# Value copies by ScalarE and early score pairs inside the projections of a decoder layer

## The reference, cut to what matters

```python
result, ch_bias, n = _chunk_decompose(hidden_states)   # chunks of 64 rows: int4 values, per-channel bias
def proj(w_orig, w_dq_t, b):                           # w_dq_t: int4 weight, one scale s for an output channel
    y = result @ w_dq_t + ch_bias @ w_orig.T
    return y.reshape(-1, H)[:n] + b
Q = (proj(q_weight, WQ, q_bias) * scaling);  K = proj(k_weight, WK, k_bias);  V = proj(v_weight, WV, v_bias)
attn = jnp.einsum('bqhd,bkhd->bhqk', Q, K)
probs = jax.nn.softmax(attn, axis=-1)
...                                                    # probs @ V, then the output projection, quantised again
```

## Time and profile before

| what | value |
|---|---|
| median of the runs | 1018.01 us |
| the profiled execution | 1018.22 us, span 1016.2 us |
| PE busy | 769.0 us (76%) |
| DVE busy | 803.1 us (79%) |
| ACT busy | 603.2 us (59%) |
| POOL busy | 85.5 us (8%) |

### The profile page before, as it was taken

How to read it: one execution, slowest core, us unless ns; L and a number is a source line. 1 busy time by engine, 2 the same in 40 slices (tenths; PEclk the granted TensorE clock), 3 DMA queues, 4 the chain that set the end, 5 groups by cost and what they waited for, 6 DMA issues and landing times.

```text
span 1016.2 us, 15370 instructions
## 1 busy us (share of the span) xinstructions
PE 769.0 (76%) x5167; PEld 320.0 (31%) x5167; DVE 803.1 (79%) x1099; ACT 603.2 (59%) x1002; POOL 85.5 (8%) x204
## 2 busy tenths in 40 slices
PE   1548895999999999999963643555555539999997
PEld 0422231222222222222221113433434424444443
DVE  7899999899999999999599998868977884622111
ACT  5829231798888888888804513765666665853000
POOL 1210001000000000001000000000000340000101
PEclk9868897799999999999985675767766859999999
DMA  8500384121212111211030000200002940000000
GB/s 293 203 1 1 124 276 148 39 56 50 59 49 58 51 55 50 56 50 50 19 132 0 1 0 4 75 25 21 1 12 94 331 148 8 1 0 1 32 21 32
DMA packets 45732, 66.69 MB, mean 66 GB/s; under 512 B 8940, under 2 KB 23276, under 8 KB 45176
## 3 DMA queue, kind: packets, MB, share of 16 engines
q1 hardware_dynamic: 44408, 61.92, 19.0%
q0 software_dynamic: 1280, 4.20, 1.3%
HBM read 42.50 MB, written 19.14 MB: 61 GB/s over the span
## 4 chain that ended last, share of the span: by engine, by line
PE 49%; DVE 27%; ACT 11%; issue 6%; DMA 3%; POOL 1%; SPq 0%; ACTq 0%; POOLq 0%; DVEq 0%
PE PS L1364 11%; PE PS L1573 8%; PE PS L1584 8%; PE PS L1381 6%; PE PS L1333 6%; ACT slab L1681 4%; PE PS L1300 2%; PE PS L1501 2%; DVE SWV L883 2%; ACT HB L1672 2%; DMA slab<-in_L_ffn_w 2%; DVE mn L716 2%; DMA slab<-in_x 1%; DVE slab L809 1%; DVE slab L808 1%
## 5 line engine op out<-in xcount | busy, mean ns | idle before, releaser
L1681 ACT ACTIVATE slab<-PS 128x512 f32<-128x512 f32 x512 | 275.9, 595 | 58.8 <-PE PS L1381 51.3
L883 DVE TENSOR_REDUCE SWV<-PS 128x2 f32<-128x1024 f32 x256 | 300.6, 1217 | 12.6 <-PE PS L1333 10.2
L1364 PE MATMUL PS<-slab,HB 128*32 128x256 f32 x2048 | 164.3, 393 | 9.9 <-ACT HB L1672 9.6
L1381 PE MATMUL PS<-slab 50*128 50x512 f16 x512 | 125.3, 387 | 2.5
L1333 PE MATMUL PS<-slab 48*128 48x512 f16 x512 | 104.3, 404 | 11.2 <-DVE SWV L883 10.2
L1573 PE MATMUL PS<-slab 128*128 128x512 f16 x384 | 86.0, 387 | 1.7 <-DVE slab L1187 1.4
L1584 PE MATMUL PS<-slab 128*128 128x512 f16 x384 | 83.0, 379 | 0.0
L1364 PEld LDWEIGHTS PS<-slab,HB 128*32 128x32 f32 x2048 | 41.6, 108 | 91.1 <-issue 64.9
L1219 DVE SCALAR_TENSOR_TENSOR WOT<-PS,cmax,WOT 128x512 f32<-128x512 f32 x8 | 6.0, 750 | 69.8 <-PE PS L1584 69.8
L1333 PEld LDWEIGHTS PS<-slab 48*128 48x128 f16 x512 | 24.7, 93 | 114.0 <-issue 95.7
L1213 DVE SCALAR_TENSOR_TENSOR slab<-HB,cmax,slab 128x512 f16<-128x512 f32 x32 | 23.8, 750 | 43.6 <-ACT slab L1778 43.6
(11 more groups left out here) (308 smaller groups left out, 1194.7 us busy)
## 6 DMA issues: line engine op xcount, KB each, us to landing
slab<-in_L_ffn_w SPq DMA_DIRECT2D x2, 4096.0 KB, 14.8
q_split<-slab SPq DMA_DIRECT2D x24, 256.0 KB, 2.7
k_split<-slab SPq DMA_DIRECT2D x24, 256.0 KB, 2.7
slab<-q_split SPq DMA_DIRECT2D x64, 96.0 KB, 2.5
slab<-k_split SPq DMA_DIRECT2D x64, 96.0 KB, 2.5
slab<-in_x SPq DMA_DIRECT2D x4, 1024.0 KB, 12.1
slab<-HB SPq DMA_DIRECT2D x128, 32.0 KB
slab<-in_fside_BxS2xS SPq DMA_DIRECT2D x4, 1024.0 KB, 5.6
```

What stands on the lines that cost most here:

```text
L883: nc.vector.tensor_reduce(NM[:, ring].rearrange("p (a x) -> p a x", a=2)[:, :, x], PS[:, bank:bank + 2, :], AX.X, ALU.max, negate=True).th ...
L1364: ins = nc.tensor.matmul(PS[32 * h:32 * h + 32, 6, cols], VST[:, r % 2, k, h, :], PROB[:, k, h, cols], start=k == half == 0, stop=k == KB ...
L1381: nc.tensor.matmul(PS[:, st_bank(2 * s + a), :], KP[rows, r, p, P * k:P * k + P], QP[rows, r, p, :], start=True, stop=True).then_inc(st_re ...
L1681: nc.scalar.activation(PROB[:, k, 2 * a + p], PS[:, st_bank(t), :], ACT.Exp, scale=score_scale).then_inc(probs, 1)
```

## The change

- The value copy of each unit goes from VectorE to ScalarE, behind its split. It multiplies by the chunk's scale only. The channel scale goes into the context's normalisation, which becomes an operation with a scalar column (`scalar_tensor_tensor`). `SWV` as a row of scales is no longer made; its space still holds the maxima, and `identh` too, which VectorE now makes ahead of the projections.
- The 15 score pairs go into the projections: none in units 0 to 4, one in units 5 to 10, two in 11 to 14, one in 15 (`PAIRS_AT`). A unit's first pair stands ahead of its query/key matmuls, the second behind them; VectorE's maxima stand the same way around its scaling. All of them use banks 4 and 5, so a pair waits until the one before is reduced.
- For that the queries and keys have two bank pairs instead of three: unit u waits until unit u - 2 is scaled, not u - 3.
- Item 0's maxima are turned in unit 14, into bank 7.
- SyncE loads items 0 and 1 behind the stores of unit 2 instead of 4.

```diff
-        identh = slab[2][:, 0:64].bitcast(F16)
...
+        identh = SWV[:, 208:272].bitcast(F16)
...
         def qk_banks(u):
-            return 2 * (u % 3)
+            return 2 * (u % 2)
+        EARLY_BANK, TURN_BANK = 4, 7
+        EARLY_PAIRS = [(n // 8, n % 8) for n in range(8 + FIRST)]
+        PAIRS_AT = [0] * 5 + [1] * 6 + [2] * 4 + [1]
+        TURN_AT = 14
+        def early_pairs(u):
+            first = sum(PAIRS_AT[:u])
+            return list(enumerate(EARLY_PAIRS))[first:first + PAIRS_AT[u]]
...
             for u in range(NT):
                 store_split(u)
-                if u == 4:
+                if u == 2:
                     sp.wait_ge(kp_ready, 1)
...
-                if m >= 2:
-                    diagonal(DGS[:, m - 2], sw[:, m], dg_ready)
+                if m == 3:
+                    diagonal(DGS[:, 0], sw[:, m], dg_ready)
...
-                dve.wait_ge(swi_out, 3)
+                dve.wait_ge(swi_out, 1)
...
+            nc.vector.tensor_copy(identh, identf[:, :]).then_inc(identh_ready, 1)
+            def maxima_of_pair(j, x, ring, bank):
+                dve.wait_ge(s_ready, 8 * j + x + 1)
+                nc.vector.tensor_reduce(NM[:, ring].rearrange("p (a x) -> p a x", a=2)[:, :, x], PS[:, bank:bank + 2, :], AX.X,
+                                        ALU.max, negate=True).then_inc(s_free, 1)
+                if x == 7:
+                    dve.wait_ge(s_free, 8 * j + 8)
+                    nm = NM[:, ring].rearrange("p (a x) -> p a x", a=2)
+                    wait(dve, mt_ready, j)
+                    nc.vector.tensor_scalar(MS_PARTS[:, 0], nm, 1.0 / ROW_UNIT, None, ALU.mult).then_inc(ms_ready, 1)
+                    dve.wait_ge(ms_ready, 2 * j + 1)
+                    nc.vector.scalar_tensor_tensor(MS_PARTS[:, 1], nm, 1.0 / ROW_UNIT, MS_PARTS[:, 0], ALU.mult,
+                                                   ALU.subtract).then_inc(ms_ready, 1)
+            def turned_maxima(j, ring, bank):
+                dve.wait_ge(mt_ready, j + 1)
+                wait(dve, mrow_in[ring % 2], 16 * (j - ring % 2))
+                nc.vector.tensor_copy(MT[:, ring % 2], PS[0:32, bank, 0:64].bitcast(F16)).then_inc(mt_copied, 1)
             def rest(u):
                 dve.wait_ge(qk_h, u + 1)
                 nc.vector.tensor_tensor(SPLIT[:, u % 3, 1], XF[u % 3], SPLIT[:, u % 3, 0], ALU.subtract).then_inc(qk_l, 1)
             for u in range(NT):
                 half, m, o = u // 8, u % 2, u % 8 // 2
+                early = early_pairs(u)
+                for _, (j, x) in early[:1]:
+                    maxima_of_pair(j, x, j, EARLY_BANK)
                 dve.wait_ge(qk_mm, u + 1)
                 if u >= 3:
                     dve.wait_ge(qk_l, u - 2)
                 ps = PS[:, qk_banks(u):qk_banks(u) + 2].rearrange("p a (n k) -> p (a n) k", k=CHUNK)
                 nc.vector.tensor_tensor(by_chunk(XF[u % 3]), ps, bc(AQ[:, m, o, 16 * half:16 * half + 16]),
                                         ALU.mult).then_inc(qk_scaled, 1)
-                dve.wait_ge(v_mm, u + 1)
-                nc.vector.scalar_tensor_tensor(V[:, u // KB, :, u % KB], PS[:, 6 + u % 2].rearrange("p (g c) -> p g c", g=NG),
-                                               s0col[:, u:u + 1], SWV[:, :].rearrange("p (g c) -> p g c", g=NG),
-                                               ALU.mult, ALU.mult).then_inc(v_scaled, 1)
+                for _, (j, x) in early[1:]:
+                    maxima_of_pair(j, x, j, EARLY_BANK)
+                if u == TURN_AT:
+                    turned_maxima(0, 0, TURN_BANK)
                 if u:
                     rest(u - 1)
             rest(NT - 1)
-            dve.wait_ge(v_scaled, NT)
-            nc.vector.tensor_copy(identh, identf[:, :]).then_inc(identh_ready, 1)
...
-            maxima(-2, -2)
-            maxima(-1, -1)
...
-                nc.vector.tensor_tensor(CTX[:, n], CTX[:, n], PS[:, NORM_BANKS[n]], ALU.mult).then_inc(norm_done, 1)
+                nc.vector.scalar_tensor_tensor(CTX[:, n], CTX[:, n], sw[:, 2, n % CT:n % CT + 1], PS[:, NORM_BANKS[n]],
+                                               ALU.mult, ALU.mult).then_inc(norm_done, 1)
...
-            pe.wait_ge(dg_ready, 2)
-            for n in range(2):
-                nc.tensor.matmul(PS[:, 4 + n, :], ones[:, :], DGS[:, n], start=True, stop=True).then_inc(swrow_ready, 1)
+            pe.wait_ge(dg_ready, 1)
+            nc.tensor.matmul(PS[:, 4, :], ones[:, :], DGS[:, 0], start=True, stop=True).then_inc(swrow_ready, 1)
...
-            pe.wait_ge(swi_out, 3)
...
+            def score_pair(j, x, ring, bank):
+                if x == 0:
+                    pe.wait_ge(qk_in[ring], j * (64 // RING) + (64 - 64 // RING * ring))
+                p, t = x // 4, x % 4
+                for a in range(2):
+                    rows = slice(LOW * a, LOW * a + MROW)
+                    ins = nc.tensor.matmul(PS[:, bank + a, :], QP[rows, ring, p, P * t:P * t + P], KP[rows, ring, p, :],
+                                           start=True, stop=True)
+                ins.then_inc(s_ready, 1)
+            def turned_in(j, bank):
+                pe.wait_ge(ms_ready, 2 * j + 2)
+                nc.tensor.transpose(PS[0:32, bank, 0:64].bitcast(F16), MS, identh).then_inc(mt_ready, 1)
+            def early_scores(n, j, x):
+                wait(pe, s_free, n)
+                score_pair(j, x, j, EARLY_BANK)
+            def scores(i, r, lo, hi):
+                for j, ahead, x, n in pairs(i, lo, hi):
+                    wait(pe, s_free, 8 * j + x - 1)
+                    score_pair(j, x, (r + ahead) % RING, SBANKS[x % 2])
             for u in range(NT):
                 half, m, o = u // 8, u % 2, u % 8 // 2
                 if u == 8:
                     pe.wait_ge(q_dve, 2)
                     pe.wait_ge(q_act, 1)
-                if u >= 3:
-                    pe.wait_ge(qk_scaled, u - 2)
+                early = early_pairs(u)
+                for n, (j, x) in early[:1]:
+                    early_scores(n, j, x)
+                if u >= 2:
+                    pe.wait_ge(qk_scaled, u - 1)
                 for q in range(2):
                     for i in range(CT):
                         nc.tensor.matmul(PS[:, qk_banks(u) + q, :], WB[:, m, i, P * o:P * o + P], QT[:, 2 * half + q, i],
...
                     ins = nc.tensor.matmul(PS[:, qk_banks(u) + q, :], CBP[32 * b:32 * b + PARTS, m, P * o:P * o + P],
                                            hot[32 * b:32 * b + PARTS, :], start=False, stop=True)
                 ins.then_inc(qk_mm, 1)
+                for n, (j, x) in early[1:]:
+                    early_scores(n, j, x)
+                if u == TURN_AT:
+                    pe.wait_ge(identh_ready, 1)
+                    pe.wait_ge(v_scaled, u)
+                    turned_in(0, TURN_BANK)
+                if u == TURN_AT + 1:
+                    pe.wait_ge(mt_copied, 1)
                 if u >= 2:
                     pe.wait_ge(v_scaled, u - 1)
...
-            scores(-2, -2, 0, 8)
-            scores(-1, -1, 0, TURN_STEP + 1)
-            pe.wait_ge(identh_ready, 1)
-            turn_maxima_of(0, -1)
-            scores(-1, -1, TURN_STEP + 1, 8)
...
-            for n, row in enumerate((SWV, SWO)):
-                act.wait_ge(swrow_ready, n + 1)
-                nc.scalar.activation(row[:, :], PS[:, 4 + n], ACT.Copy).then_inc(swi_out, 1)
+            act.wait_ge(swrow_ready, 1)
+            nc.scalar.activation(SWO[:, :], PS[:, 4], ACT.Copy).then_inc(swi_out, 1)
...
                 nc.scalar.activation(SPLIT[:, u % 3, 0], XF[u % 3], ACT.Copy).then_inc(qk_h, 1)
+                act.wait_ge(v_mm, u + 1)
+                nc.scalar.activation(V[:, u // KB, :, u % KB], PS[:, 6 + u % 2].rearrange("p (g c) -> p g c", g=NG), ACT.Copy,
+                                     scale=s0col[:, u:u + 1]).then_inc(v_scaled, 1)
```

More of the change, by code:

```diff
@@ L576, in _ @@
             pool.wait_ge(swi_ready, 3)
-            pool.wait_ge(swrow_ready, 2)
+            pool.wait_ge(swrow_ready, 1)
             nc.gpsimd.memset(KP[:, :, :, :], ROW_UNIT).then_inc(kp_ready, 1)
@@ L874, in _ @@
             rest(NT - 1)
[L875 to L876 removed]
             def maxima(i, r):
                 for j, ahead, x, n in pairs(i):
[L881 to L893 removed]
+                    maxima_of_pair(j, x, (r + ahead) % RING, SBANKS[x % 2])
                     if n == TURN_STEP and exists(i + 1):
[L895 removed]
+                        turned_maxima(i + 1, (r + 1) % RING, STBANK[TURN % 3])
                 if isinstance(i, int) and i == NI - 2:
[L897 to L905 removed]
+                    turned_maxima(i + 1, (r + 1) % RING, STBANK[TURN % 3])
             steps(dve, maxima)
@@ L919, in bias_parts @@
             def bias_parts():
-                dve.wait_ge(swi_out, 4)
+                dve.wait_ge(swi_out, 3)
                 chunk_bias_parts(2, PS[:, 7:8], SWIO.unsqueeze(1), CBPO.unsqueeze(1))
@@ L1320, in _ @@
             pe.wait_ge(v_scaled, NT)
```

(15 more changed lines are left out.)

18 lines of the change are left out of this document (removed).

## The result

The changed kernel took 1028.91 us (median of 4 runs, 1027.19 to 1031.36) against 1017.99 us for the kernel before on the same chip: a ratio of 1.0108, 95% interval [1.0081, 1.0134]. Run again later, it took 1028.67 us (6 runs, 1027.47 to 1032.32), ratio 1.0091 [1.0065, 1.0116]. It is slower by some 9 to 11 us. The larger figure owes something to its baseline: over 71 later runs on three chips the kernel before lay in three groups, near 1017.5, 1019.4 and 1022.3, while the four runs with the median 1017.99 lie at its lower end (1017.85 to 1018.71). The forecast was 1025.3 (1017 to 1031), slower. The profiled execution took 1027.19 us, its span is 1025.1, 8.9 more than before.

A forecast was written before the change was run, and what follows sets the result against it. TensorE was taken to set the projections' pace, and item 0's start to move the kernel's end. Item 0 later by 6.9 plus 0.6 in the normalisation made +7.5 on 1018.01, given as 1025.3 us, range 1017 to 1031.

The forecast's parts named there:

- Step 1: Start of the projections: two bank pairs leave TensorE idle 5.1 us before unit 2, then low clock; unit 5 scaled +2.45.
- Step 2: Unit 5: the first early pair waits 3.9 us for item 0's load, then low clock +2.1; sum so far +8.8.
- rival A: Unit 5's wait brings no low clock, or two-pair units have a shorter chain: +3.6 us, 1021.6; chance 18%.
- Step 3: Projection units with pairs: 3.76 us apart with one (+1.9 in all), 4.96 with two (+6.1); unit 15 scaled at 174.6.
- Step 4: Value copies on ScalarE in the projections: TensorE asks for them two units on, 6.9 us later, so they cost nothing.
- rival E: Projections: ScalarE's copy holds up the values, each unit by up to 1 us: +5 more, 1030 us; chance 6%.
- Step 5: From last scaling to item 0: stores land, then maxima are sent, 11.1 us; item 0 at 185.7, +6.9.
- Step 6: Context's normalisation: operations with a scalar column take longer, 12 on the chain at 0.055 each: +0.6 us.
- The sum: Whole kernel: +6.9 at item 0's start and +0.6 in the normalisation make +7.5 us.
- B: TensorE keeps its high clock from the projections into item 0: +1.6 us, 1019.6; chance 14%.
- C: Item 0 is loaded when unit 5 asks, no wait: -0.8, or -2.6 with VectorE's pace in two-pair units, 1015.4; chance 10%.
- D: Low clock in the two-pair units, 2.5 us longer in each of four: +10 us, 1035; chance 7%.

The follow-up runs named there:

- e9: The changed kernel as it is, run again later: 1028.67 us, ratio 1.0091 to the kernel before.
- e2: Changed kernel with the first early pair in unit 6 instead of 5 and two pairs in units 10 to 14: 1023.78 us, ratio 1.0032 to the kernel before.
- e7: Kernel before with two bank pairs for queries and keys instead of three, nothing else: 1023.30 us, ratio 1.0026.
- e1: Kernel before with value copies on ScalarE and the channel scale in the normalisation, three bank pairs, pairs not moved: 1023.44 us, ratio 1.0021.
- e8: Changed kernel with first pair in unit 6, item 0's maxima sent early and three bank pairs up to unit 4: 1014.79 us, ratio 0.9956 to the kernel before.
- e3: Changed kernel with item 0's maxima sent behind unit 13's stores and ScalarE's wait for landed stores moved into item 0: 1021.60 us, ratio 1.0015 to the kernel before.
- e14: e1 with the value copies of units 0 and 1 put ahead of ScalarE's first split: 1017.26 us, ratio 0.9981 to the kernel before.
- e12: e8 with the value copies of units 0 and 1 put ahead of ScalarE's first split: 1012.38 us, ratio 0.9927 to the kernel before.
- e13: e12 with one pair in each of units 6 to 15 and the last five pairs behind the projections: 1012.55 us, ratio 0.9927 to the kernel before.

## Why the prediction was right, step by step

- **Step 1** (start of the projections, +2.45): right. TensorE idle for 5.95 us in the profile of after, 0.76 of it that execution's own, and 4.99 in e9 (forecast 5.1). Unit 3 scaled at 118.50 and 118.70 (the forecast says 118.95, its own terms add up to 118.86), unit 5 of e2 at +2.24, and e7 alone gives +2.3.
- **Step 2** (wait of unit 5): right in mechanism and size. First early pair at 127.17 after 3.98 us (127.5 after 3.9), e9 127.23 after 3.85. The low clock behind it came as well, eight matmuls in 3.27 and 3.59 us. Sum behind it 8.0, and 8.6 in e9 (unit 5 at 131.94), where 8.8 was forecast. That the prediction priced the low clock by TensorE's idleness of step 1, and not at nothing, decided between the forecast and rival A.
- **Step 3** (units with pairs): 3.76 apart with one pair as forecast, 5.00 with two (4.96). Last scaling 173.92 (174.6). The ring through the one bank pair sets the pace rather than an engine, by the waits of the trace: VectorE was busy 13.99 of 15.00 us, TensorE 12.68. No run gave the early pairs a second bank pair.
- **Step 4** (values on ScalarE, nothing): **wrong at the start**, right elsewhere. I looked at plain units, where the copy has 6.9 us, and not at the first, where it stands behind a split that waits for VectorE. In the changed kernel the wait of step 1 for VectorE's scaling covers it (nothing is added there), so the total came out all the same, by luck in this step. e1 shows +2.4 without that cover, e8 that it takes the place of step 1's wait as soon as that is gone. It was rival E's kind of mechanism, put in the wrong units.
- **Step 5** (stores and maxima): right. Stores to landing 176.30 to 182.73, 6.4 (5.8); sending 2.9 (3.0); item 0 at 185.61 (185.7). That it came within 0.1 us is luck: the last scaling was 0.7 early and the way from it to item 0, 11.7 us, 0.6 longer than forecast, and in e9 item 0 began at 186.59. e3 confirms the mechanism by taking it away.
- **Step 6** (normalisation, +0.6): right. 746 ns an operation against 686, so 0.060 each (the prediction used 0.055, where its two rows give 0.064), and the shift grows from +6.0 at the last exponential (514.8 against 508.8) to +6.6.
- **The sum** (+7.5): 6.6 at the normalisation, made of 6.8 at item 0, 0.8 that came back between item 0 and its last exponential (+6.0), and the 0.6. Most of the 0.8 is the clock: the first eight context matmuls at full speed (0.64 us) start 11.2 us behind item 0's first pair, 11.9 before, and the prediction had no term for that. The rest up to the measured 9 to 11 is behind the normalisation, in code that the change does not touch, which the prediction took to cost the same in every execution. Its sum also has a slip: 1018.01 and 7.5 make 1025.5, and 1025.3 takes the 0.2 off twice. And its range holds the kernel before as well (1018), so being inside it says little; the places and the sizes of the waits say more.

Of the rivals, A would have needed a clock that does not fall behind unit 5 and two-pair units 4.51 apart, which were 5.00; B a high clock at item 0, which ran its first 10.6 us at 0.50; C loads 3.9 us earlier (e2 shows its gain from the other side, by asking later). D did not come: in the two-pair units the granted clock was 1.00 over the whole 15 us, with TensorE busy 85% and cut by a wait for the bank pair every 5 us. The failure that the Trainium skill describes (TensorE: Matmul & The Clock Gate, "A second HAM failure mode: psum-queue depth-cycling") was not seen here with waits of 0.64 to 0.85 us.

## What to carry to other kernels

Moving work into a stage with room is half of the job: what used to hide behind that work (here the landing of stores and an 8 KB message that was sent only behind them) is then bare, and the first consumer placed too early stalls everything behind it in its engine's order. Look at the first and last rounds of a loop separately, since queue positions that are harmless in the middle decide there. And price a stall of the matrix engine with the low clock that follows: after 2.9 to 6.4 us of idleness it ran at the low clock each time in these projections, at once or within 1.2 us, and after 1.97 us it did not.

## What was not expected of the hardware

- The same place, three lengths of idleness: after 1.97 us TensorE went on at full speed (e14: four matmuls in 1.04); after 2.94 the four took 1.75 and the next eight 2.56 (e12); after 4.41 the next eight took 3.59 (e1). Shortening the stall of e1 by 2.4 us was worth 5.5 at the last scaling. But the length alone does not set the price: after 3.33 us (e13) the four took 1.89 and the eight 3.59, just as after 4.41, and after 3.39 in the kernel before 1.17 and 3.14.
- The same code behind the last normalisation operation took 484.0 to 489.5 us from profile to profile, and TensorE 324.9 to 332.7 for the same 1620 matmuls; the two do not go together in every profile. Effects of 2 us need ten runs a side here, and better still the position of a late instruction in the trace.
- The value copy from PSUM, 128x512 in fp32 with a scale from a column, took ScalarE 0.67 us, against 0.75 for VectorE's with the row of scales.
